# Degree counts by one-hot products: ids split into 5 low and 7 high bits in place of 7 and 5

## The reference

```python
idx = jnp.concatenate([edge_index, edge_index[:, ::-1]], axis=0)
src, dst = (idx[:, 0], idx[:, 1])
...
m = jax.ops.segment_max(score, src, num_segments=N)
denom = jax.ops.segment_sum(ex, src, num_segments=N)
...
deg = jax.ops.segment_sum(jnp.ones((src.shape[0],), h_e.dtype), dst, num_segments=n)
inv_deg = (1.0 / jnp.maximum(deg, 1.0))[:, None]
```

## Time and profile before

| | |
|---|---|
| median of 3 runs | 6148.54 us (6140.91 to 6149.28) |
| the profiled execution | 6139.35 us, its span 6137.6 us |
| busy: TensorE, DVE, ACT, POOL | 2661.9, 4092.7, 1253.9, 3783.2 us |
| mean granted TensorE clock | 0.604 of full speed |
| degree loop on DVE | first L1049 at 186.3 us, last at 430.4 us |
| record stores on POOL | 784 of L695, 866.1 us busy |
| gathers on POOL | 2592 of L738, 2685.8 us busy |

### The profile page before, as it was taken

How to read it: one execution, slowest core, us unless ns; L and a number is a source line. 1 busy time by engine, 2 the same in 40 slices (tenths; PEclk the granted TensorE clock), 3 DMA queues, 4 the chain that set the end, 5 groups by cost and what they waited for, 6 DMA issues and landing times.

```text
span 6137.6 us, 56339 instructions
## 1 busy us (share of the span) xinstructions
PE 2661.9 (43%) x13332; PEld 1809.3 (29%) x13333; DVE 4092.7 (67%) x6865; ACT 1253.9 (20%) x4370; POOL 3783.2 (62%) x3760
## 2 busy tenths in 40 slices
PE   1785101011332322222222342677674577777746
PEld 0661101011322222222222242546453232332315
DVE  9778888886986776767676774232322576676655
ACT  0000000000111111111111110000000677777741
POOL 2777777776777777777777774000002777777730
PEclk6555555555555555555555555767685788888876
DMA  6221121211222222222222231435261222332230
GB/s 229 53 54 51 48 56 48 73 29 50 77 79 61 72 61 71 63 70 64 69 64 68 66 85 39 144 104 179 69 205 22 58 83 77 87 86 77 84 98 7
DMA packets 388365, 472.44 MB, mean 77 GB/s; under 512 B 212478, under 2 KB 248384, under 8 KB 381041
## 3 DMA queue, kind: packets, MB, share of 16 engines
q1 hardware_dynamic: 132624, 279.73, 13.8%
q0 software_dynamic: 114832, 129.82, 9.7%
q10 hardware_dynamic: 140752, 61.28, 3.5%
HBM read 291.34 MB, written 179.19 MB: 77 GB/s over the span
## 4 chain that ended last, share of the span: by engine, by line
POOL 58%; issue 21%; PE 9%; DMA 6%; DVE 5%; ACT 0%; POOLq 0%; DVEq 0%; ACTq 0%; SPq 0%
POOL arena L738 44%; POOL rec_dram L695 11%; PE acc L1959 4%; DMA oh<-mt_dram 2%; PE acc L1780 2%; DMA V<-in_edge_attr_dram 2%; DMA rec_dram<-V,rowst 1%; PE acc L1782 1%; PE acc L1943 1%; POOL own_dram L715 1%; POOL pdum L688 1%; POOL arena L765 1%; DVE arena L1579 1%; PE pt L1770 0%; POOL own_dram L769 0%
## 5 line engine op out<-in xcount | busy, mean ns | idle before, releaser
L738 POOL DMA_INDIRECT arena<-tab_dram,jst x2592 | 2685.8, 1036 | 778.3 <-issue 777.8
L695 POOL DMA_INDIRECT rec_dram<-V,rowst x784 | 866.1, 1105 | 229.9 <-issue 217.8
L688 POOL TENSOR_TENSOR pdum<-pdum 128x1 f32<-128x1 f32 x197 | 58.5, 297 | 1138.3 <-DVE arena L1607 864.6
L1902 PE MATMUL pw<-OHX 128*128 128x128 bf16 x1632 | 210.3, 310 | 1120.8 <-DVE OHX L1414 1120.8
L1902 PEld LDWEIGHTS pw<-OHX 128*128 128x128 bf16 x1632 | 156.9, 140 | 1172.3 <-DVE OHX L1414 859.7
L1910 PE MATMUL acc<-arena,oh 128*128 128x64 f32 x1952 | 427.1, 420 | 20.9 <-DVE oh L1423 20.7
L1910 PEld LDWEIGHTS acc<-arena,oh 128*128 128x128 f32 x1952 | 417.2, 330 | 34.9 <-issue 34.9
L900 ACT ACTIVATE arena<-arena,ew 128x64 f32<-128x64 f32 x1728 | 417.8, 333 | 33.3 <-PE acc L1983 33.3
L1437 DVE TENSOR_TENSOR arena<-arena,pt 128x1024 f32<-128x1024 f32 x108 | 131.8, 1221 | 431.7 <-DMA arena<-tab_dram,jst 429.4
L900 ACT ACTIVATE OHX<-arena,ew 128x64 f32<-128x64 f32 x1728 | 417.7, 333 | 2.5
L1983 PE MATMUL acc<-OHX,ident 128*128 128x512 f32 x432 | 253.7, 753 | 371.0 <-ACT OHX L900 371.0
(11 more groups left out here) (523 smaller groups left out, 6463.2 us busy)
## 6 DMA issues: line engine op xcount, KB each, us to landing
oh<-mt_dram SPq DMA_DIRECT2D x90, 512.0 KB, 3.6
arena<-tab_dram,jst POOLq DMA_INDIRECT x2592, 2.5
arena<-rec_dram SPq DMA_DIRECT2D x122, 288.0 KB, 3.6
mt_dram<-oh ACTq DMA_DIRECT2D x272, 128.0 KB, 1.7
oh<-mt_dram SPq DMA_DIRECT2D x75, 416.0 KB, 3.9
oh<-mt_dram SPq DMA_DIRECT2D x75, 384.0 KB, 4.0
rows_dram<-V SPq DMA_DIRECT2D x27, 1056.0 KB, 4.0
rows_dram<-arena SPq DMA_DIRECT2D x27, 1056.0 KB, 4.3
```

The source lines that it names most:

```text
L695: gp.indirect_dma_start(rec[:, :], bass.IndirectOffsetOnAxis(ap=rowst[:, q, k:k + 1], axis=0), recst[:, q, k, :], None).then_inc(S[f"scat{ ...
L738: gp.indirect_dma_start(hd.G[:, a.r, j, :], None, table[:, :], row_of(jst[:, a.r, j:j + 1])).then_inc(S[f"{x}g{a.r}"], 16)
L1902: last = nc.tensor.matmul(unit_bank(c.slot)[:, k // 2 * P:(k // 2 + 1) * P], mones[c.slot][:, 0, k, :], mones[c.slot][:, 1, k, :], start=k ...
```

## The change

An id is now split into x = its low 5 bits and h = its high 7 bits (h = 4 c + m, with m the two bits between). Both arrays lie side by side in one operand: `dlo` is 2 x 32 wide, `dhi` 2 x 100 wide. A step makes them with two comparisons, one of 128 x 2800 and one of 128 x 896, and TensorE takes two matmuls a column: `dhi` of destinations by `dhi` of sources (100 x 100, into `pu`), and all of `dlo` by all of `dhi` (64 x 200, into `accw`), of which the two blocks on the diagonal are the degrees. Behind the loop the degrees are put together by eight small copies, and the 100 x 100 pair counts are brought down to 25 x 25 by one reduction on DVE and one more matmul. Ids beyond the last edge get h = 127.

```diff
@@
-NCW = NC + NC % 2
+DL, DH = 32, 4 * NC
@@
-        lo2, bk2 = [[cols(k + l).bitcast(BF).rearrange("p (j e) -> p j e", e=2) for l in range(2)] for k in (8, 10)]
+        lo2, hi2 = [arena[0:EP, k * EC:(k + 2) * EC].bitcast(BF).rearrange("p (j l e) -> p j l e", l=2, e=2) for k in (8, 10)]
@@
-        dgo = OHX[0:EP, 1024:1024 + 4 * KP * (NCW + P)].rearrange("p (q f) -> p q f", q=2)
-        dhi = dgo[:, :, 0:2 * KP * NCW].rearrange("p q (l k n) -> p q l k n", l=2, n=NCW)
-        dlo = dgo[:, :, 2 * KP * NCW:2 * KP * (NCW + P)].rearrange("p q (l k n) -> p q l k n", l=2, n=P)
+        dgo = OHX[0:EP, 1024:1024 + 4 * KP * (DL + DH)].rearrange("p (q f) -> p q f", q=2)
+        dlo = dgo[:, :, 0:2 * KP * DL].rearrange("p q (k x) -> p q k x", k=KP)
+        dhi = dgo[:, :, 2 * KP * DL:2 * KP * (DL + DH)].rearrange("p q (k x) -> p q k x", k=KP)
@@
             for l in range(2):
-                for o, values in ((lo2[l], lof[l]), (bk2[l], bkf[l])):
-                    link(V.tensor_copy(o, values.unsqueeze(2).to_broadcast([EP, EC, 2])))
+                link(V.tensor_copy(key_i[0], idf[l]))
+                link(V.tensor_scalar(key_i[1], key_i[0], 5, None, ALU.logical_shift_right))
+                link(V.tensor_scalar(key_i[0], key_i[0], DL - 1, None, ALU.bitwise_and))
+                link(V.tensor_copy(hi2[:, :, l], key_i[1].unsqueeze(2).to_broadcast([EP, EC, 2])))
+                link(V.tensor_copy(lo2[:, :, l], key_i[0].unsqueeze(2).to_broadcast([EP, EC, 2])))
+                for a, e, c in ((0, EX, EF + 1), (EX, 2 * EX, EF), (2 * EX, P, EF)):
+                    link(V.memset(hi2[a:e, c:EC, l], 127.0))
@@
                 after(v, S["dgm"], i * 2 + q - 1)
-                part = [0]
-
-                def ones_of(o, values, wide, a, n):
-
-                    k = bass.ds((i * 2 + q) * KP + a, n)
-                    V.tensor_tensor(paired(o[:, a:a + n]), iota_pairs(n, wide, EP),
-                                    values[:, k, :].unsqueeze(2).to_broadcast([EP, n, wide // 2, 2]), ALU.is_equal).then_inc(S["dg"], 1)
-                    part[0] += 1
-                    v.wait_ge(S["dg"], i * 12 + q * 6 + part[0])
-                for l in range(2):
-                    ones_of(dhi[:, q, l], bk2[l], NCW, 0, KP)
-                    ones_of(dlo[:, q, l], lo2[l], P, 0, KP // 2)
-                    ones_of(dlo[:, q, l], lo2[l], P, KP // 2, KP // 2)
+                k = bass.ds((i * 2 + q) * KP, KP)
+                for part, (o, values, wide) in enumerate(((dhi, hi2, DH), (dlo, lo2, DL))):
+                    V.tensor_tensor(paired(o[:, q].rearrange("p k (l n) -> p (k l) n", l=2)), iota_pairs(2 * KP, wide, EP),
+                                    values[:, k].rearrange("p j l e -> p (j l) e").unsqueeze(2).to_broadcast([EP, 2 * KP, wide // 2, 2]),
+                                    ALU.is_equal).then_inc(S["dg"], 1)
+                    v.wait_ge(S["dg"], i * 4 + q * 2 + part + 1)
@@
-            link(V.tensor_copy(degf[:, 0:NC], accw[:, 0:NC]))
-            link(V.tensor_copy(degf[:, NC:2 * NC], pt[:, 0:NC]))
+            for l in range(2):
+                for m in range(4):
+                    link(V.tensor_copy(degf[m * DL:(m + 1) * DL, l * NC:(l + 1) * NC],
+                                       accw[l * DL:(l + 1) * DL, l * DH:(l + 1) * DH].rearrange("p (c m) -> p c m", m=4)[:, :, m]))
+            fours, four_i, four_of = lcol[:, 550:550 + NC], lcol[:, 600:601], lcol[:, 601:602]
+            link(V.tensor_reduce(fours[0:DH], pu[0:DH, 160:160 + DH].rearrange("p (c m) -> p c m", m=4), AX, ALU.add))
+            link(V.tensor_scalar(four_i.bitcast(I), pidx_i[:, 7:8], 2, None, ALU.logical_shift_right))
+            link(V.tensor_copy(four_of, four_i.bitcast(I)))
+            link(V.tensor_scalar(lcol[:, 625:625 + NC], iota[:, 0:NC], four_of, None, ALU.is_equal))
@@
-            count = pu[0:NC, 160:160 + NC]
+            count = acc[0:NC, 512:512 + NC]
@@
-                pe.wait_ge(S["dg"], 12 * i + 6 * q + 6)
+                pe.wait_ge(S["dg"], 4 * i + 2 * q + 2)
                 for k in range(KP):
                     st_ = isinstance(i, int) and i == 0 and q == 0 and k == 0
-                    nc.tensor.matmul(pu[0:NC, 160:160 + NC], dhi[:, q, 0, k, 0:NC], dhi[:, q, 1, k, 0:NC], start=st_, stop=True, skip_group_check=True)
-                    nc.tensor.matmul(accw[:, 0:NC], dlo[:, q, 0, k, :], dhi[:, q, 0, k, 0:NC], start=st_, stop=True, skip_group_check=True)
-                    last = nc.tensor.matmul(pt[:, 0:NC], dlo[:, q, 1, k, :], dhi[:, q, 1, k, 0:NC], start=st_, stop=True, skip_group_check=True)
+                    nc.tensor.matmul(pu[0:DH, 160:160 + DH], dhi[:, q, k, 0:DH], dhi[:, q, k, DH:2 * DH], start=st_, stop=True, skip_group_check=True)
+                    last = nc.tensor.matmul(accw[0:2 * DL, 0:2 * DH], dlo[:, q, k], dhi[:, q, k], start=st_, stop=True, skip_group_check=True)
                 last.then_inc(S["dgm"], 1)
@@
             nc.tensor.matmul(acc[:, 0:50], triinc[:], lcol[:, 50:100], start=True, stop=True)
+            nc.tensor.matmul(acc[0:NC, 512:512 + NC], lcol[0:DH, 625:625 + NC], lcol[0:DH, 550:550 + NC], start=True, stop=True)
```

## The result

The changed kernel takes **6322.65 us** (median of four executions, 6310.73 to 6323.69), against 6146.02 for the kernel before: a ratio of 1.0284, with a 95% interval of 1.0271 to 1.0297. It is 177 us slower, where 26 were forecast; the time lies far above the range of 6146 to 6208. The profiled execution took 6310.73 us, 171 more than that of before.

A forecast was written before the change was run, and what follows sets the result against it. POOL's march to the key loads was taken to bound the kernel: 37 us more in the degree loop, 11 us less after the sorts, +26 us on 6148.5, so 6174 us, with a range of 6146 to 6208.

The forecast's parts named there:

- What bounds the kernel now: Whole kernel: POOL's march from its first record store to 1468 us sets the end; DVE has 33.51 us idle.
- DVE's step: Degree loop: comparisons of 1.62 and 0.63 us, a pair of steps 5.56 us, the loop 156 us, 92 less.
- Around the loop: Before and behind the degree loop: extra small operations, 4.5 and some 3 us more on DVE, none on the path.
- TensorE's step: Degree loop: weight loads hidden, 3.5 us a step at 1.2 GHz, 1.75 at 2.4; 2.4 taken, DVE sets the pace.
- POOL beside the new loop: Degree loop: long comparisons hold POOL's record stores, 84 go through in place of 109, 37 us more on the path.
- What comes back: After the sorts, which end earlier at 1352: POOL issues 85 instructions beside an idle DVE, 11 us less.
- if DVE is late at the keys: Fetch of the sorted keys: sign of a wrong forecast, which expected DVE idle ahead of them for 140 us.
- Rival 4: Degree loop: TensorE's loads don't hide, 387 ns a column, loop 303 us, POOL waits 42 us: 6190; chance 0.04.
- Rival 1: Degree loop: number of comparisons, not length, holds POOL; down to -30 us, 6118; chance 0.09, of which 0.06 faster.
- Rivals 2 and 3: Degree loop: two stores fit a 3.0 to 3.2 us step, 6150 to 6160, chance 0.17; one store, 6210, chance 0.13.

The follow-up runs named there:

- two loops: Changed kernel with each step's fourteen pair-count matmuls first, then its fourteen degree matmuls, weights unaltered: 6163.96 us, ratio 1.0036.
- both 128, split: Changed kernel with both weight operands 128 columns wide and the comparison of 2800 elements made in four pieces: 6138.66 us, ratio 0.9989 to before.
- two loops, split: Changed kernel with pair-count matmuls before degree matmuls in each step and the 2800-element comparison in four pieces, no padding: 6137.12 us, ratio 0.9989 to before.
- the experiment on the kernel before: Kernel before with the pair-count matmul's 25-column weights replaced by 128 columns, true pair counts left out: 6147.05 us in one execution, against 6142.25.

## Why the prediction failed

The instant at which block 3's indices arrive (the third row of POOL above; 1497.68 us before) against the difference of the medians in the same job:

| kernel | indices there | later by | time, against before |
|---|---|---|---|
| changed kernel | 1676.60 | +178.9 | +176.6 |
| pair-count weights 128 | 1633.97 | +136.3 | +135.9 |
| both 128 | 1521.71 | +24.0 | +20.9 |
| degree weights 128 | 1521.72 | +24.0 | +23.5 |
| degree weights 66 | 1521.55 | +23.9 | +29.4 |
| two loops | 1520.34 | +22.7 | +21.7 |
| both 128, split | 1491.16 | -6.5 | -6.3 |
| two loops, split | 1492.88 | -4.8 | -5.1 |

The last two columns agree within 3 us, but for the weights of 66 columns (5.5 us).

*What bounds the kernel now* was right as a rule: POOL's march sets the end unless DVE comes late to the keys, and nothing behind that place gives back or adds much.

*DVE's step* was right: 1.63 and 0.63 us forecast as 1.62 and 0.63; where TensorE kept up, the loop took 157 us against 156 and the third sort ended at 1354 against 1352.

*Around the loop* was right within 2 us; it lies on DVE alone.

***TensorE's step* is the step that failed.** It took "14 x 300 / 1.2 = 3.5 us at 1.2 GHz", with both loads hidden, and then the clock of 2.4 GHz. Measured: 7.8 us at 1.2 GHz, to the loop's end. The hiding was read off 50 matmuls that all had weights of 128 columns, and carried over to weights that alternate between 100 and 64. The sum is right for weights of one sort: 250 ns a column, measured in three kernels. The misreading had begun a line above it, where the kernel before was called "bound by loading weights": the earlier trace rows has one column's length, and the rows shown with the experiment on the kernel before have 0.13, 0.05 and 0.11 us between its starts, of which the two long ones are the changes from 25 columns to 128 and back. Two unequal gaps in front of loads of 128 columns asked for a reason, and I gave none.

*POOL beside the new loop* and *What comes back* were right, but of a kernel that the change did not make. With the loads hidden, 86 stores went through the 157 us, for 84 forecast, the last started at 1276.6 for 1275, and the four kernels with the whole comparison and hidden loads stood 21 to 29 us above before, for 26. In the changed kernel itself none of this reached the end: POOL came to its fetch at 1470.5 and waited; the prediction had named that as a sign of being wrong, "if DVE is late at the keys".

*Rival 4* is what happened, with a chance of 0.04. Its wait and its point of decision held, though not its reason: loads of 100 and of 64 columns do hide, each among its own kind. DVE lost 196.8 us; less the 21 between 1437 and 1458, and with 2.8 for writing the keys, that is 178.6, and 178.9 was measured at the indices. Its price was too low: it gave the loads their column count at 1.2 GHz, (100 + 64 + 300) / 1.2 = 387 ns, where they took 160 and 128 ns and a column 555. Its chance was too low because it asked for a general failure to hide, against which the later stage did speak; that the failure could depend on what stands next to the load was in no rival.

*Rival 1* is out (the hold goes by the length of the operation). *Rivals 2 and 3* had no occasion.

## What to carry to other kernels

Before alternating matmuls in one stream, look at the number of weight columns of each: in this kernel every change between weights of 64 (or 25) columns and of 66 or more cost 105 to 150 ns. Put those of one sort behind one another, or add idle columns to the narrow ones; with either, this kernel came out as with both operands at 128 columns, within the intervals. When a row is used as proof that a cost is hidden, the shapes *around* it belong to the proof. And where GpSimd issues indirect DMAs beside VectorE, several comparisons of half a microsecond can be better than one of 1.6: they were here, by 27 us in both pairs of kernels.

## What was not expected of the hardware

- The change of width, by the starts of the matmuls at 1.2 GHz: 555 ns a column for 100 and 64 weight columns, 500 for 128 and 64, and 250 for 128 and 128, 100 and 128, and 100 and 66. With two changes to a column that is (555 - 250) / 2 = 152 and (500 - 250) / 2 = 125 ns for each, and 105 in the kernel before; single changes read 0.14 and 0.13 us in the two kernels with two loops. What the switch goes by is open in one point: the columns of the weights are also the rows of PSUM that a matmul writes, and no run here tells the two apart. The Trainium skill describes in "TensorE: Matmul & The Clock Gate", section "Packing small matmuls — row/col tiling", that the array is addressed in tiles and that a load can be pulled ahead where it does not conflict. Whether weights of 64 columns are put into another tile than wider ones, and whether that is what costs the time, no run here shows. Whether 25 and 64 columns are of one sort was not tried.
- In the two kernels whose loads don't hide, loads show as 103 ns for 128 columns, 128 for 64 and 160 for 100; where they hide, the same shapes show as anything from 95 to 208 ns, and 128-column weights changed every 27 ns in the kernel before with all three at 128. The Trainium skill's same page, section "Weight-path perf modes — Fast Weight Load (FWL) and DoubleRow", has a faster load for weights of exactly 128 columns; the records agree (103 ns for 128 columns against 160 for 100). Where the loads don't hide, that difference of 57 ns is what 128 and 64 (500 ns) gain on 100 and 64 (555 ns); where they hide it changed nothing: 100 beside 128 or 66 ran at 250 ns as 128 beside 128 did.
- The granted clock stayed at 0.50 for 439 us in which TensorE showed as 100% busy and streamed 250 of 555 ns, and for the loop of 128 and 64 (250 of 500). In the three kernels with a column of 250 ns and the whole comparison it was 0.50 between 191 and 195 us and 1.00 between 200 and 348. So the serial loads came with the lower clock; how much of the 7.8 us a step is the clock's, no run here separates.
